# Transposes, root chains and waits placed elsewhere in a transformer stack on one NeuronCore

## The reference

```python
def attn_layer(x, Wqkv, qs, ksc, Wo):          # windowed stack, 16 heads of 64
    q, k, v = split(x @ Wqkv)
    q = l2norm(q) * qs;  k = l2norm(k) * ksc   # 1/sqrt(sum of squares) per head and token
    q, k = rotary(q), rotary(k)
    out = softmax(q k^T * 8, over this window of 32 and the one before) v
    return out @ Wo
x = attn_layer(shift_tokens(x)) + x;  x = ffn_layer(shift_tokens(x)) + x     # six times

# latent attention, 16 heads of 8
q_c, k_c, v = small projections of x;  q_c, k_c = rms_norm(q_c) * w, rms_norm(k_c) * w
out = softmax(causal(q k^T / sqrt(8))) v, then an output projection
```

## Time and profile before

| | |
|---|---|
| median of three runs | 6266.62 us (6263.59 to 6266.95) |
| profiled execution, its own time | 6259.03 us |
| its span, first to last instruction | 6257.3 us |
| mean granted TensorE clock | 0.95 of full speed |
| busy, share of the span | PE 87%, PEld 61%, DVE 68%, ACT 63%, POOL 43% |
| one windowed turn | 46.65 us, 96 of them, about 4480 us |
| latent attention | from about 5388 to 5704 us of the span |

### The profile page before, as it was taken

How to read it: one execution, slowest core, us unless ns; L and a number is a source line. 1 busy time by engine, 2 the same in 40 slices (tenths; PEclk the granted TensorE clock), 3 DMA queues, 4 the chain that set the end, 5 groups by cost and what they waited for, 6 DMA issues and landing times. The chain is left out here.

```text
span 6257.3 us, 121573 instructions
## 1 busy us (share of the span) xinstructions
PE 5454.5 (87%) x41154; PEld 3791.3 (61%) x41154; DVE 4256.5 (68%) x16112; ACT 3942.9 (63%) x11510; POOL 2699.1 (43%) x2578
## 2 busy tenths in 40 slices
PE   7885799999999999997489999999999999687989
PEld 5673466666666666665256666666666666454678
DVE  4453777777777877875477777787787777444522
ACT  2211677777777778774177777777777877221333
POOL 0000555555555555552165555555555555220000
PEclk9996899999999999998599999999999999787999
DMA  0000000000000000000000000000000000000000
GB/s 11 22 1 2 21 1 15 6 11 9 7 10 6 11 9 11 8 1 4 21 1 10 9 3 11 9 11 9 1 15 6 11 8 1 5 2 4 2 28 8
DMA packets 30964, 53.45 MB, mean 9 GB/s; under 512 B 7688, under 2 KB 17168, under 8 KB 29712
## 3 DMA queue, kind: packets, MB, share of 16 engines
q1 hardware_dynamic: 30352, 45.66, 2.3%
HBM read 44.60 MB, written 1.05 MB: 7 GB/s over the span
## 5 line engine op out<-in xcount | busy, mean ns | idle before, releaser
L1785 PE MATMUL bank<-wA,next_rowT 128*128 128x512 f32 x2304 | 1185.6, 624 | 272.7 <-DVE turnB L2126 164.0
L1982 ACT ACTIVATE pairs<-pairs,negmax 128x128 f32<-128x128 f32 (+1 forms) x3072 | 1240.4, 420 | 19.0 <-DVE negmax L2087 15.6
L1959 POOL TENSOR_TENSOR turnA<-raw,ropes 128x512 f32<-128x512 f32 x768 | 968.7, 1272 | 243.8 <-ACT raw L2006 214.8
L2087 DVE CUSTOM_DVE_ANT_0 pairs<-bank,bands,big 128x128 f32<-128x128 f32 (+1 forms) x3072 | 941.4, 362 | 86.4 <-PE bank L1717 82.9
L1966 POOL TENSOR_TENSOR qk<-turnA,turnB 128x512 f32<-128x512 f32 x768 | 976.9, 1272 | 0.0
L1785 PEld LDWEIGHTS bank<-wA,next_rowT 128*128 128x128 f32 x2304 | 377.1, 190 | 719.2 <-DVE turnB L2126 378.9
L1943 POOL COPY spread<-recip 128x256 f32<-128x256 f32 x768 | 305.7, 398 | 965.0 <-DVE recip L2096 958.0
L1972 POOL TENSOR_TENSOR qk<-qk,big 128x1024 f32<-128x1024 f32 x192 | 365.6, 1904 | 739.0 <-DVE recip L2201 739.0
L1989 ACT ACTIVATE pairsT<-bank 128x512 f32<-128x512 f32 x768 | 469.2, 611 | 337.3 <-PE bank L1730 337.1
L1982 ACT ACTIVATION_READ_ACCUMULATOR pairs<-pairs,negmax 128x1 f32 x3072 | 631.2, 205 | 0.0
L285 POOL TENSOR_TENSOR rstd<-vareps,neg_half 128x2 f32<-128x2 f32 x56 | 39.0, 696 | 1287.1 <-DVE vareps L256 888.0
(11 more groups left out here) (306 smaller groups left out, 11229.7 us busy)
## 6 DMA issues: line engine op xcount, KB each, us to landing
wA<-in_wt_wqkv SPq DMA_DIRECT2D x72, 256.0 KB, 2.8
wB<-in_wt_wo SPq DMA_DIRECT2D x12, 512.0 KB, 3.5
wC<-in_wt_w SPq DMA_DIRECT2D x12, 341.0 KB, 2.9
wD<-in_wt_w SPq DMA_DIRECT2D x12, 192.0 KB, 2.4
big<-in_e_up SPq DMA_DIRECT2D x1, 2048.0 KB
big<-in_e_down SPq DMA_DIRECT2D x1, 2048.0 KB
scl<-in_wt_scales SPq DMA_DIRECT2D x12, 128.0 KB, 3.1
X<-in_x SPq DMA_DIRECT2D x8, 128.0 KB, 2.5
```

The lines of the kernel that those rows point to most:

```text
L1785: pe.matmul(side_bank(i)[:, :], c.next_rowT[:, t * P:(t + 1) * P], wqkv[:, k * 512:(k + 1) * 512], start=True, stop=True).then_inc(s.chunk ...
L1959: g.tensor_tensor(c.turnA[:, m % 2, :].rearrange("p (h d) -> p h d", h=8), c.raw[:, m % 4, :].rearrange("p (h d) -> p h d", h=8), cos, ALU ...
L1982: last = a.activation(tile, tile, ACT.Exp, scale=-1.0, bias=c.negmax[:, 2 * p + side, t:t + 1], accum_out=c.pair_sums[:, p % 4, t, side:si ...
L2087: last = v.tensor_tensor_reduce(c.pairs[:, 2 * (p % 4) + side, AT[t]:AT[t] + SPAN[t]], c.bank[side][:, AT[t]:AT[t] + SPAN[t]], c.bands[:, ...
```

## The change

In the windowed stacks `pe_shares` moves up, from behind the scores to directly behind `pe_turn_probs`, in all slots. The first chain of roots moves from slot 3 to slot 2, where it stands at the end, behind the feed-forward statistics. In the latent attention `turn_qk`, `copy_qk` and `pick` leave the second half of a loop turn and stand at the head of the next one; `turn_row` and `norm.scalar` go behind `flipped(b, 0)` and its exponential; the maximum of unit 6 is taken before `scale_qk`; and the waits on the bank `side` are rewritten for the new order. No arithmetic instruction is added or removed.

```diff
@@ -1355,9 +1355,7 @@
             pe.wait_ge(blocks_ready, 1)
 
             def turn_row(b):
-                if ok(b - 2):
-                    pe.wait_ge(core.neg_ready, core.before + b - 1)
-                elif ok(b - 1):
+                if ok(b - 1):
                     pe.wait_ge(core.k_ready, core.before + b)
                 norm.transpose(pe, b)
 
@@ -1370,8 +1368,8 @@
 
             def turn_qk(b):
                 pe.wait_ge(normed, b + 1)
-                if ok(b - 3):
-                    pe.wait_ge(added, b - 2)
+                if ok(b - 1):
+                    pe.wait_ge(core.neg_ready, core.before + b)
                 for which in range(2):
                     for t in range(HALVES):
                         last = pe.transpose(side[:, (2 * which + t) * P:(2 * which + t + 1) * P], qk[which][:, t, :],
@@ -1382,6 +1380,8 @@
                 pe.wait_ge(core.ctx_ready, core.before + b + 1)
                 if ok(b + 3):
                     pe.wait_ge(squared, 2 * (b + 3) + 2)
+                elif ok(b + 2):
+                    pe.wait_ge(core.k_ready, core.before + b + 3)
                 elif ok(b + 1):
                     pe.wait_ge(core.neg_ready, core.before + b + 2)
                 else:
@@ -1391,10 +1391,10 @@
                 last.then_inc(ctx_in_psum, 1)
 
             def maxima(b):
-                if ok(b + 1):
-                    pe.wait_ge(core.k_ready, core.before + b + 2)
+                if ok(b - 2):
+                    pe.wait_ge(added, b - 1)
                 else:
-                    pe.wait_ge(added, b - 1)
+                    pe.wait_ge(squared, 2 * (b + 2))
                 core.turn_maxima(pe, core.before + b, side)
 
             def scores(b, a):
@@ -1410,9 +1410,11 @@
                     core.weigh(pe, core.before + b, j)
 
             for b in range(-2, B + 1):
+                if ok(b + 1):
+                    turn_qk(b + 1)
+                flipped(b, 0)
                 if ok(b + 2):
                     turn_row(b + 2)
-                flipped(b, 0)
                 scores(b + 1, 0)
                 weigh(b - 1, 3)
                 if ok(b + 2):
@@ -1431,8 +1433,6 @@
                 weigh(b, 1)
                 scores(b + 1, 5)
                 scores(b + 1, 6)
-                if ok(b + 2):
-                    turn_qk(b + 2)
                 flipped(b, 3)
                 scores(b + 1, 7)
                 weigh(b, 2)
@@ -1466,15 +1466,15 @@
                 a.activation(core.kT(core.before + b), side[:, S:2 * S], ACT.Identity).then_inc(core.k_ready, 1)
 
             for b in range(-2, B + 1):
-                if ok(b + 2):
-                    norm.scalar(a, b + 2)
+                if ok(b + 1):
+                    copy_qk(b + 1)
                 for j in range(4):
                     if ok(b):
                         core.exp(a, core.before + b, j)
+                    if ok(b + 2) and j == 0:
+                        norm.scalar(a, b + 2)
                     if ok(b + 2) and j < HALVES:
                         copy_projection(b + 2, j)
-                    if ok(b + 2) and j == 2:
-                        copy_qk(b + 2)
                 if ok(b + 1):
                     core.copy_maxima(a, core.before + b + 1, side[:, 0:S])
 
@@ -1528,6 +1528,9 @@
                 v.tensor_tensor(qk[1], scaled[:, :, D:2 * D], proj[:, :, 2 * D:3 * D], ALU.add).then_inc(normed, 1)
 
             for b in range(-2, B + 1):
+                if ok(b + 1):
+                    v.wait_ge(q_ready, b + 2)
+                    core.pick(v, core.before + b + 1)
                 take_max(b + 1, 0)
                 if ok(b - 1):
                     core.finish(v, core.before + b - 1)
@@ -1540,16 +1543,12 @@
                     add(b - 1)
                 if ok(b + 3):
                     norm.statistics(v, b + 3, step)
-                take_max(b + 1, 4, 5)
+                take_max(b + 1, 4, 5, 6)
                 if ok(b + 2):
                     scale_qk(b + 2)
-                take_max(b + 1, 6)
+                take_max(b + 1, 7)
                 if ok(b + 3):
                     norm.normalise(v, b + 3)
-                take_max(b + 1, 7)
-                if ok(b + 2):
-                    v.wait_ge(q_ready, b + 3)
-                    core.pick(v, core.before + b + 2)
 
 
 
@@ -1615,7 +1614,7 @@
 PE_LATE_QKT_SLOTS = {0: (4, 5), 3: (6, 7)}
 COPY_LATE_QKT_SLOTS = {0: 2, 3: 3}
 DVE_ROTATE_SLOTS = {1: (0, 1), 2: (2, 3), 4: (4, 5), 5: (6, 7)}
-DVE_RSQRT_SLOTS = {3: 0, 6: 1}
+DVE_RSQRT_SLOTS = {2: 0, 6: 1}
 POOL_SLOTS = {1: ("cos0", "cos1", "add0"), 2: ("cos2", "add1", "cos3", "add2"), 3: ("add3", "scale0"),
               4: ("cos4", "cos5", "add4"), 5: ("cos6", "add5", "cos7", "add6"), 6: ("add7", "scale1")}
 
@@ -1889,6 +1888,10 @@
             following = has_turn(T + 1)
             for p in range(PAIRS):
                 pe_turn_probs(pe, T, p)
+                if p >= 1:
+                    pe_shares(pe, T, p - 1)
+                elif has_turn(T - 1):
+                    pe_shares(pe, T - 1, PAIRS - 1)
                 if p + 2 < PAIRS:
                     pe_scores(pe, T, p + 2)
                 elif following:
@@ -1896,10 +1899,8 @@
                 if p == 0 and following:
                     pe_xT(pe, T + 1)
                 if p >= 1:
-                    pe_shares(pe, T, p - 1)
                     pe_weigh(pe, T, p - 1)
                 elif has_turn(T - 1):
-                    pe_shares(pe, T - 1, PAIRS - 1)
                     pe_weigh(pe, T - 1, PAIRS - 1)
                 for i in PE_LATE_QKT_SLOTS.get(p, ()):
                     pe_turn_qk(pe, T, i)
```

## The result

The changed kernel takes 6112.89 us (median of 4 runs, 6105.19 to 6121.37), the kernel before 6265.35 in the same session: a ratio of 0.9757 (95% interval 0.9740 to 0.9774), 152 us less. The forecast was 6134 us, range 6085 to 6205. The profiled execution is the slowest of the four: 6121.37 us, span 6119.5, which is 137.8 us under the span before. Where they went, by the marks of VectorE's addition at the end of each turn: 60.4 us in the first windowed run (first to last mark 2130.5 before, 2070.1 now), 63.3 in the second (2067.2), 23.3 behind it, where the latent attention is; ahead of the first mark 2.8 were lost and between the runs 6.4. I forecast 102 for the windowed runs and 31 for the latent attention.

The account below looks back on a forecast made before the run. The windowed turn of 46.64 us was taken as the bound. 102 us from the windowed runs and 31 from the latent attention turned 6259.0 into 6126 us; the median lies 7.6 higher, so 6134 us, range 6085 to 6205.

Parts of the forecast that it names:

- What bounds the kernel: The windowed turn of 46.64 us, 96 turns in two runs: 0.1 us per turn is worth some 10 us.
- Part 1: Windowed slots: shares directly behind the probabilities, one pause of 0.17 us from scores to weighing, weighing 0.17 us earlier.
- The two bounds: Scores to weighing: no pause would gain 0.34 us, a double pause 0.
- Part 2: Roots in slot 2: VectorE's 0.84 us of waits go, last rotation 1.01 us earlier, TensorE stands 2.1 us before chunk 7.
- nothing of GpSimd runs beside the roots: Slot 2: GpSimd's next instruction behind the statistics waits for slot 3's reciprocal, which stands behind the roots.
- So ScalarE, not VectorE, sets the end of slot 5, and 0.80 of the 1.01 us comes through: Slot 5: ScalarE's 8.9 us without waits end chunk 11's copy at 1543.2 instead of 1543.98.
- Slot 6, another 0.37 us for the weighing: Slot 6: shares fit in ahead of the scores for nothing, so the weighing comes 0.37 us earlier, 1.17 in all.
- Rival (d): Slot 3: TensorE's new wait lets the clock fall, costing 1.87 us per turn, time 6306 us; chance 0.06.
- Part 3: Latent attention: the 3.57 us wait goes and the clock stays up, 5.07 us less per turn, 31 us in all.
- a `flipped` at full clock takes 2.07: Latent attention: with `turn_qk` 2.71 us at full clock instead of 4.58, so 1.87 us are the clock's.
- The sum: Whole kernel: 6259.0 - 102 - 31 = 6126 us as profiled; the median lies 7.6 above, so 6134 us.
- windowed term: Both windowed runs: 1.11 us less per turn, 46.64 to about 45.5, over 92 turns, 102 us.

Follow-up runs that it names:

- runs that relieve one or both: Changed kernel with slot 3's keys copied early (6089.28 us), with VectorE's normalisation moved from slot 4 to slot 5 (6115.01 us), or with both (6037.76 us).
- part 3 alone: The kernel before with only the latent attention changed, both windowed runs as before: 6235.89 us, ratio 0.9957.
- part 2 alone: The kernel before with only the first chain of roots moved from slot 3 to slot 2: 6186.56 us, ratio 0.9874.

## Why the prediction was right, and where not

**What bounds the kernel**: right. A few tenths of a us per turn were the whole result.

**Part 1, one pause of 0.17**: right, in the rows to 0.02 us. The two bounds (no pause, a double pause) are out. TensorEngine Tiling (Array Packing) in the Trainium skill, Key Properties, has it so: a change of mode drains TensorE, and going from scores to weighing is one change (0.17 us).

**Part 2, the waits of VectorE are gone and chunk 7 waits 2.1 us**: right (2.17). Slot 4 was to start 1.4 us late and started 1.08 late; slot 5 was to be 0.2 early and was 0.57 early. One sentence of this part is wrong: that nothing of GpSimd runs beside the roots. The last addition of slot 2 does, and holds their first instruction up for about 1.0 us. It did not show in the sum, because the same addition had held up the instruction before it in the kernel before; that is luck.

**"So ScalarE, not VectorE, sets the end of slot 5, and 0.80 of the 1.01 us comes through"**: this term failed, by 0.5 us per turn, 48 in all. From the second probabilities' load of slot 7 the copy of chunk 11 ends 36.63 us later (1072.04 less 1035.41), before it was 37.95 (1543.98 less 1506.03): 1.32 us came through. Three things were mis-sized. VectorE's own gain was 1.31 us at chunk 11's load, not 1.01. Of the 0.30 between them 0.23 is there when the chain ends: before, the last instruction of the statistics took 1.25 us, held up until GpSimd's addition ended at 1527.73; now it starts at 1055.55, 0.07 us ahead of that addition, takes 0.17, and the chain's first instruction is the one held up, for 1.18. The hold-up ends at the same point of the turn, but for the 0.17 of slot 1, and one instruction fewer stands behind it. Another 0.05 lies between slot 3's reciprocal and the key copy, 1.95 us (1059.47 to 1061.42) for the 2.00 that I took: without a wait ahead of it, the copy starts before the last minima end. ScalarE got chunk 7 0.3 us sooner than forecast and needed 8.72 us for what I put at 8.9; with that it is level with VectorE. The runs that relieve one or both show the tie, so the step "ScalarE, not VectorE" is half right. SBUF — State Buffer in the Trainium skill, Who interferes with whom, says that VectorE and GpSimd share a pair of ports under an exclusive lock which such a tensor_scalar can take, and that the issue order decides who blocks; the rows agree: 1.18 and 0.18 us for the same instruction with and without the addition beside it, and 1.25 or 0.17 us by which of the two started first.

**Slot 6, another 0.37 us for the weighing**: right. The turn from slot 6 to slot 7 is 0.38 us shorter.

**Rival (d), the clock falls in the stop of slot 3**: I gave it 0.06, all or nothing, at 1.87 us. The mechanism is real and was weighed against the wrong yardstick: that the waits of 1.35 and 0.89 us leave the clock full said nothing of 2.17; and the rival speaks of a stop of 1.7 us where part 2 has 2.1. It hit 20 of 88 turns at 1.3 us, some 27 us. The changed kernel's four runs spread over 16 us where the kernel before spreads over 3 in the same session; that the hits do this isn't shown, since in other sessions the kernel before spreads over 6.5 to 13.7 us, with no such turn in the profile kept of it. TensorE: Matmul & The Clock Gate in the Trainium skill, HAM oscillation, has the clock fall in each round of a loop, but its loop has longer waits than this stop, so its rule doesn't give the 6306 us that the prediction takes from it. Here the clock fell in every fourth round at 2.17 us, and in two of three at 2.97.

**Part 3, 5.07 us per latent turn**: the wait of 3.57 us went as forecast, and no wait came at `maxima`. The clock did not stay up. The step "a `flipped` at full clock takes 2.07" counted the whole fall as the long wait's, and the stop of 1.35 us ahead of scores 6, which was there before, is followed by a fall of its own in four of seven turns once the long wait no longer comes behind it. A row of the kernel before pointed that way: the long wait began at 5508.55 (5512.12 less 3.57), and the clock was down within 1 us of it, so that its whole length wasn't needed:

```profile
5509.00:5510.00 1.00, 0.00 (x0) 0.00 (x0) 0.00 (x0) 0.00 (x0) 1.00 (x1) 0.74 0.00 0
```

With the fall a turn gains 3.9 us, six turns 23 us. In the one turn without it the gain is 5.7, more than I had; what the further 0.6 are I haven't traced.

**The sum**: 5 us short in the profiled execution, by errors that offset each other; that it came so near is luck. The windowed term missed 48 us on one side and 27 on the other by the clock, the latent one 8. What happens ahead of and between the runs, 9 us more than before, is most likely scatter: in the kernel with part 3 alone, whose windowed parts are the same as before, it is 6 us more as well (2 ahead and 4 between), and over the profiles of all kernels here the first mark lies between 759.0 and 769.0 us and the stretch between the runs between 314.6 and 325.0. So no profile tells the sum to better than some 10 us.

## What to carry to other kernels

When a step is moved ahead on one engine, list the copies that another engine waits for behind it, and put those first: here one line, the key copy ahead of the slot's reciprocal, shares, transposes and minima, was worth 24 us, and it opened the way for 51 more. When two engines are level, price each gain with the other's slack, and try both reliefs together before giving one up. A stop of the matrix engine costs nothing by itself if it is paid back later, but it may cost the clock behind it; compare its length with stops in the same trace that left the clock full, and treat anything longer as open, with a cost of its own in part of the rounds.

## What was not expected of the hardware

- The same stop of 2.17 us lets the granted clock fall in one turn and not in the next. The hits often lie 136.2 or 181.3 us apart, three or four turns; so it matters when the stop comes, and not only how long it is. With part 2 alone a stop only 0.11 us shorter (2.06) was never followed by such a turn, though there the turn is 0.78 us longer too, and no run tells the two apart.
- A fall costs nearly the same each time, 1.3 us per windowed turn, whether the stop is 2.17 or 2.97 us.
- An instruction of VectorE held up by GpSimd isn't marked as a wait: it shows as a long duration (1.18 us for one that else takes 0.18). Taking it away only showed the next wait, of 0.91 us. Which of the two engines stands is decided by hundredths of a us: 0.03 too late cost VectorE 1.08 us, 0.06 ahead cost it nothing.
